# Graph attention with ELU and layer norm on one core: other group sizes, earlier loads, a shorter decode and another order at the end

## What is computed

```python
Wh = x @ W;  We = entity_embs @ W
scores = (Wh @ a1)[:, None] + (We @ a2)[None, :]
e = where(scores > 0, scores, 0.2 * scores)
e = where(adj > 0, e, -9e15)
h = softmax(e, axis=1) @ entity_embs + x
x = layernorm(x + elu(h), axis=-1)
```

## Time and profile before

| | |
|---|---|
| median of 3 runs | 354.25 us (353.78 to 355.08) |
| profiled execution: time | 353.8 us |
| profiled execution: span | 351.7 us |
| busy share of the span: TensorE, VectorE, ScalarE, GpSimd | 80%, 84%, 72%, 12% |
| first fused operation (line 542) starts | 65.57 us |
| last of the 128 is done | 333.48 us |

### The profile page before, as it was taken

The page is one execution under the profiler, slowest core; times in us unless marked ns, Lnnn a source line. Parts: engine busy times, 40 slices in busy tenths (PEclk is TensorE's granted clock), DMA queues, the critical chain, the costliest instruction groups (busy, mean ns, idle before and its releaser), DMA issues.

```text
span 351.7 us, 7943 instructions
## 1 busy us (share of the span) xinstructions
PE 280.9 (80%) x3470; PEld 142.3 (40%) x3470; DVE 296.7 (84%) x356; ACT 253.6 (72%) x216; POOL 40.9 (12%) x45
## 2 busy tenths in 40 slices
PE   1249675779999989999999999999959696667730
PEld 1146454535445544455445445545423232212210
DVE  1780523799988989999999999999999999999944
ACT  1087563399888949999999899999837764646620
POOL 6011110001101000000000310000040000002201
PEclk9998999699999999999999999999999999999985
DMA  7999999999999968887989591000000000000000
GB/s 149 257 207 208 207 207 207 207 208 206 207 175 187 151 101 126 136 131 120 152 140 145 85 173 32 2 3 2 2 0 32 3 0 2 0 2 0 32 0 30
DMA packets 34817, 37.23 MB, mean 106 GB/s; under 512 B 672, under 2 KB 33504, under 8 KB 34784
## 3 DMA queue, kind: packets, MB, share of 16 engines
q0 software_dynamic: 33280, 33.56, 59.0%
q1 hardware_dynamic: 1504, 3.18, 3.2%
HBM read 69.24 MB, written 1.05 MB: 200 GB/s over the span
## 4 chain that ended last, share of the span: by engine, by line
PE 32%; issue 22%; DVE 21%; DMA 13%; ACT 9%; POOL 2%; POOLq 1%; DVEq 0%; ACTq 0%
PE acc L749 12%; DMA raw<-adj_dram 12%; DVE xm L534 10%; PE pairs L698 10%; PE acc L752 6%; DVE wts L542 5%; ACT mask L321 5%; ACT wts L335 3%; PE hist L714 3%; POOL rstd L278 1%; DVE mask L523 1%; PE misc L729 1%; DMA w_sb<-weights_in_dram 1%; ACT drow L351 1%; POOL raw L272 1%
## 5 line engine op out<-in xcount | busy, mean ns | idle before, releaser
L335 ACT ACTIVATE wts<-wts,q_bias 128x1024 f32<-128x1024 f32 x128 | 143.5, 1150 | 45.1 <-DVE wts L542 44.4
L542 DVE SCALAR_TENSOR_TENSOR wts<-pb,q_bend,xm 128x1024 f32<-128x1024 f32 x128 | 160.5, 1279 | 2.0 <-PE acc L752 1.8
L749 PE MATMUL acc<-wts,ent_sb 128*32 128x512 f32 x1024 | 135.4, 601 | 16.8 <-ACT wts L335 13.1
L321 ACT ACTIVATE mask<-pairs 128x2048 bf16<-128x2048 bf16 x53 | 99.0, 1875 | 28.9 <-PE pairs L698 28.9
L698 PE MATMUL pairs<-ident,raw 128*128 128x128 bf16 x1024 | 71.3, 226 | 13.2 <-DMA raw<-adj_dram 10.3
L534 DVE TENSOR_TENSOR xm<-mask,drow 128x2048 bf16<-128x2048 bf16 x64 | 78.1, 1220 | 2.3 <-ACT drow L351 2.3
L752 PE MATMUL acc<-wts,onesf 128*32 128x256 f32 x1024 | 78.6, 379 | 0.0
L698 PEld LDWEIGHTS pairs<-ident,raw 128*128 128x128 bf16 x1024 | 61.6, 102 | 34.3 <-issue 23.0
L752 PEld LDWEIGHTS acc<-wts,onesf 128*32 128x32 f32 x1024 | 33.1, 111 | 77.6 <-issue 77.6
L272 POOL DMA_DIRECT2D raw<-adj_dram x32 | 28.3, 884 | 173.6 <-PE pairs L698 170.9
L749 PEld LDWEIGHTS acc<-wts,ent_sb 128*32 128x32 f32 x1024 | 26.7, 109 | 42.0 <-ACT wts L335 27.9
(11 more groups left out here) (98 smaller groups left out, 101.2 us busy)
## 6 DMA issues: line engine op xcount, KB each, us to landing
raw<-adj_dram POOLq DMA_DIRECT2D x32, 1024.0 KB, 10.5
ent_sb<-ent_blocks_dram SPq DMA_DIRECT2D x1, 1024.0 KB, 7.5
x_sb<-x_dram SPq DMA_DIRECT2D x4, 256.0 KB, 8.6
out_dram<-y SPq DMA_DIRECT2D x4, 256.0 KB, 2.0
w_sb<-weights_in_dram SPq DMA_DIRECT2D x1, 32.5 KB, 2.1
```

The source lines that it names most:

```text
L321: act.activation(mask[:, i % RING:i % RING + 2, 0:n], pairs[j % 2][:, :, 0:n], ACT.Relu, scale=2.0 ** LIFT).then_inc(act_mask_done, 1)
L335: act.activation(part, part, ACT.Exp, bias=q_bias[:, b:b + 1]).then_inc(w_done, 1)
L542: dve.scalar_tensor_tensor(wts[:, i % SLOTS, 0:n], pb[:, P * TILE0[g]:P * TILE0[g] + n], q_bend[:, b:b + 1], xm[:, i % XS, 0:n], ALU.max, ...
L749: pe.matmul(acc[0][to:to + Q, 0:n], ent_sb[:, b, Q * f:Q * f + Q], part[:, n * k:n * k + n], start=(b == 0), stop=(b == NB - 1))
```

## The change

- The groups have 4, 6, 8, 8 and 6 tiles, so there are 160 steps and 40 loads. All operations of a group are as wide as its tiles. Which pairs VectorE masks changes (`by_dve`): pairs 7, 9, 11, 13, 15 of group 0, each second of group 1, pairs 1, 4, 8 and 12 of group 2. Of pair 15 ScalarE and VectorE mask one step each. The last load of the first group is split in two.
- GpSimd issues its first load without waiting for the weights.
- The decode has two operations that don't wait for each other and a minimum, where it had five in a chain; their constants are made in `q_scale` and `find_shift`. `empty` is made behind them.
- For the first group VectorE copies the row to `drow`, in place of ScalarE.
- After the last step, VectorE copies the sums out of PSUM beside ScalarE's copy of the features, takes the positive part beside the exponential, and squares by itself.

```diff
-SIZES = (8, 8, 8, 8)
+SIZES = (4, 6, 8, 8, 6)
...
-            return g == 0 and k >= 9 and k % 2 == 1 or g == 1 and k % 3 == 2 or g == 2 and k in (2, 5)
+            return g == 0 and k >= 7 and k % 2 == 1 or g == 1 and k % 2 == 1 or g == 2 and k in (1, 4, 8, 12)
+
+        def by_act(j):
+            return j == GROUP_PAIRS - 1 or not by_dve(j)
...
+                first = CHUNK // 2 if n == LATE else CHUNK
+                pool.dma_start(raw[:, n % RAWS, 0:SIZES[g], 0:P * first],
+                               rows(adj, g)[:, :, P * CHUNK * c:P * (CHUNK * c + first)]).then_inc(adj_in[n % RAWS], 16)
+                if n == LATE:
+                    pool.dma_start(raw[:, n % RAWS, 0:SIZES[g], P * first:P * CHUNK],
+                                   rows(adj, g)[:, :, P * (CHUNK * c + first):P * CHUNK * (c + 1)]).then_inc(late_in, 16)
...
-            pool.wait_ge(w_in, 16)
             load(0)
...
                 dve.wait_ge(q_step, 6)
+                dve.tensor_scalar(key_slope[:, 0:1], qstep[:, :], -1.0, None, ALU.mult)
+                dve.tensor_scalar(key_slope[:, 1:2], qstep[:, :], -ALPHA, None, ALU.mult)
...
+                dve.tensor_tensor(base_diff[:, :], shift[:, :], qbase[:, :], ALU.subtract).then_inc(shift_step, 1)
+                dve.scalar_tensor_tensor(key_base[:, :], qbase[:, :], -ALPHA, shift[:, :], ALU.mult, ALU.add).then_inc(shift_step, 1)
+                dve.wait_ge(shift_step, 5)
+                dve.tensor_scalar(p_base[:, :], pcol[:, :], ALPHA - 1, base_diff[:, :], ALU.mult, ALU.add).then_inc(shift_step, 1)
...
-                dve.tensor_scalar(empty[:, s], st[:, 3, 0:m], 1.0, None, ALU.is_le)
-                dve.tensor_scalar(st[:, 0, 0:m], st[:, 3, 0:m], qstep[:, :], qbase[:, :], ALU.mult, ALU.add).then_inc(st_step, 1)
...
+                dve.scalar_tensor_tensor(st[:, 0, 0:m], st[:, 3, 0:m], key_slope[:, 0:1], p_base[:, s], ALU.mult,
+                                         ALU.add).then_inc(st_step, 1)
+                dve.tensor_scalar(st[:, 1, 0:m], st[:, 3, 0:m], key_slope[:, 1:2], key_base[:, :], ALU.mult,
+                                  ALU.add).then_inc(st_step, 1)
                 dve.wait_ge(st_step, n + 5)
...
+                dve.tensor_tensor(dcol[:, 0:m], st[:, 0, 0:m], st[:, 1, 0:m], ALU.min).then_inc(d_done, 1)
+                dve.tensor_scalar(empty[:, s], st[:, 3, 0:m], 1.0, None, ALU.is_le).then_inc(empty_done, 1)
...
+            def finish_last():
+                dve.wait_ge(w_used, STEPS)
+                dve.wait_ge(turn_sums_mm, g)
+                dve.tensor_copy(wsum_sb[0:sums, 0:P * fourth(g)], acc[1][0:sums, 0:P * fourth(g)]).then_inc(last_wsum, 1)
+                for part in range(4):
+                    finish(g, part)
+                dve.wait_ge(att_done, NG)
+                fin_inc(dve.scalar_tensor_tensor(pos, y_g, 0.0, x_gr, ALU.max, ALU.add))
+                fin_wait()
+                dve.wait_ge(elu_done, NG)
+                fin_inc(dve.scalar_tensor_tensor(y_g, e_g, 1.0, pos, ALU.min, ALU.add))
+                for part in (6, 7):
+                    finish(g, part)
+                dve.wait_ge(centred, NG)
+                dve.tensor_tensor(e_g, y_g, y_g, ALU.mult).then_inc(square_done, 1)
+                for part in (8, 9, 10):
+                    finish(g, part)
```

More of the change, by code:

```diff
@@ L19 @@
 CHUNKS = STEPS // CHUNK
+LATE = NB // CHUNK - 1
 RAWS = 5
@@ L126, in attention_layernorm @@
         qbase = sb("qbase", [P, 1], fp32)
+        key_slope = sb("key_slope", [P, 2], fp32)
+        key_base = sb("key_base", [P, 1], fp32)
+        base_diff = sb("base_diff", [P, 1], fp32)
+        p_base = sb("p_base", [P, NT], fp32)
         empty = sb("empty", [P, NT], fp32)
@@ L193, in attention_layernorm @@
         d_done = sem("d_done")
+        empty_done = sem("empty_done")
         row_mm = sem("row_mm")
@@ L244, in by_dve @@
             g, k = divmod(j, GROUP_PAIRS)
-            return g == 0 and k >= 9 and k % 2 == 1 or g == 1 and k % 3 == 2 or g == 2 and k in (2, 5)
+            return g == 0 and k >= 7 and k % 2 == 1 or g == 1 and k % 2 == 1 or g == 2 and k in (1, 4, 8, 12)
+        def by_act(j):
+            return j == GROUP_PAIRS - 1 or not by_dve(j)
         def mask_made(engine, j):
-            engine.wait_ge(dve_mask_done if by_dve(j) else act_mask_done, sum(by_dve(k) == by_dve(j) for k in range(j + 1)))
+            if by_act(j):
+                engine.wait_ge(act_mask_done, sum(by_act(k) for k in range(j + 1)))
+            if by_dve(j):
+                engine.wait_ge(dve_mask_done, sum(by_dve(k) for k in range(j + 1)))
         @block.sync
@@ L314, in store_pair @@
                 i = 2 * j
-                if by_dve(j):
+                if not by_act(j):
                     return
@@ L320, in store_pair @@
                 n = cols(i // NB)
-                act.activation(mask[:, i % RING:i % RING + 2, 0:n], pairs[j % 2][:, :, 0:n], ACT.Relu,
+                k = 1 if by_dve(j) else 2
+                act.activation(mask[:, i % RING:i % RING + k, 0:n], pairs[j % 2][:, 0:k, 0:n], ACT.Relu,
                                scale=2.0 ** LIFT).then_inc(act_mask_done, 1)
@@ L358, in take_acc @@
                 rows_of_sums = Q * len(fourths(g))
-                act.activation(acc_sb[:, 0:P * half(g)], acc[0][:, 0:P * half(g)], ACT.Copy)
-                act.activation(wsum_sb[0:rows_of_sums, 0:P * fourth(g)], acc[1][0:rows_of_sums, 0:P * fourth(g)],
-                               ACT.Copy).then_inc(acc_free, 1)
+                features_taken = act.activation(acc_sb[:, 0:P * half(g)], acc[0][:, 0:P * half(g)], ACT.Copy)
+                if g + 1 < NG:
+                    act.activation(wsum_sb[0:rows_of_sums, 0:P * fourth(g)], acc[1][0:rows_of_sums, 0:P * fourth(g)],
+                                   ACT.Copy).then_inc(acc_free, 1)
+                else:
+                    features_taken.then_inc(acc_free, 1)
             for j in range(4):
@@ L522, in store_pair @@
                 n = cols(i // NB)
-                dve.tensor_scalar(mask[:, i % RING:i % RING + 2, 0:n], pairs[j % 2][:, :, 0:n], 2.0 ** LIFT, 0.0, ALU.mult,
-                                  ALU.max).then_inc(dve_mask_done, 1)
+                k = 1 if by_act(j) else 0
+                dve.tensor_scalar(mask[:, i % RING + k:i % RING + 2, 0:n], pairs[j % 2][:, k:2, 0:n], 2.0 ** LIFT, 0.0,
+                                  ALU.mult, ALU.max).then_inc(dve_mask_done, 1)
             def masked(j):
@@ L628, in _ @@
             decode(0)
+            take_row(0)
             dve.wait_ge(p_rows, ROWS)
@@ L644, in _ @@
                         masked(s // 2 + 1)
-            for part in range(11):
-                finish(NG - 1, part)
+            finish_last()
         @block.tensor
@@ L691, in turn_pair @@
                 pe.wait_ge(adj_in[n % RAWS], 16 * (n // RAWS + 1))
+                if j == GROUP_PAIRS - 1:
+                    pe.wait_ge(late_in, 16)
                 if j >= 2:
```

29 lines of the change are left out of this document (16 added, 13 removed).

## The result

The changed kernel takes 347.88 us (median of 4, 347.55 to 349.07) beside 354.01 for the kernel before: ratio 0.9831, 95% interval 0.9802 to 0.986. It is 1.7% faster.

What follows compares the result with a forecast made beforehand. Start and tail cost wide groups, the loop narrow ones, bounded by TensorE in groups 0 and 1, then mostly VectorE. Start -17.2, loop +21.0, tail -3.4 gave +0.4 on the 354.25 median: 354.6 us, range 349.5 to 358.5.

Steps and rivals of the forecast that it cites:

- the surcharge on the loop: Loop: TensorE-bound groups run 3% over the engine's sum; group 0 gets 2.0 over plus 0.7, group 1 gets 1.3.
- The row of a group: TensorE's sums: eight transposes of the row priced at 1.04 us, taken from the start's trace.
- The weight loads behind 128-column sums: Group 0 at 4 tiles: weight loads hide less well behind short sums, 0.7 us, bounded by nothing to 1.5.
- The prices by width: Loop: costs scaled by tiles; weighing a step takes TensorE 1.29 us at 8 tiles, 1.075 at 6, 0.645 at 4.
- The start: Before the first fused operation: it comes at 48.4 us against 65.6, so -17.2, with bounds 46.5 and 51.
- The 137: Start: hardware queue at 137 GB/s with both queues fed, so earlier adj loads make ent land at 10.4, 1.45 late.
- the half clock for two pairs: Start's upper bound, 51 us: TensorE's clock falls in the wait to 33.6, staying low for a third of remaining pairs.
- the entity sum blocks pair 7: Start: pair 7's mask stands behind the 3.87 us ent_part reduction on VectorE, to 33.6, and TensorE waits.
- The tail: After the last step: 14.8 us against 18.2, so -3.4, with bounds 14.2 and 16.
- the shorter decode: VectorE's decode in the loop falls from 2.5 to 2.1 us, included in the group sums.
- Handoffs in group 0: Slower rival: VectorE idles 6.7 us before masks, waits feed each other, group 0 takes 52, total 359.5; chance 0.25.
- The shorter start: Faster rival: ent lands at 8.93 and pairs with a row take 1.2 instead of 1.45: -3.0, total 351.6; chance 0.30.

Runs made afterwards that it cites:

- experiment 2: The changed kernel with four groups of 8 tiles and the old by_dve shares, so all but the sizes: 349.58 us, ratio 0.9866 to the kernel before.
- experiment 9: The kernel before, with VectorE masking pairs 1, 4, 7, 10, 13 of group 1 instead of 2, 5, 8, 11, 14: 353.18 us, ratio 0.9983.
- experiment 1: The kernel before with the new group sizes 4, 6, 8, 8, 6 alone: 349.48 us, ratio 0.9871 to the kernel before.
- experiment 3: The changed kernel with VectorE masking the pairs it masked before (old by_dve shares): 345.66 us, ratio 0.9777 to the kernel before.
- experiment 7: The changed kernel with the old decode, five operations in a chain and empty ahead of them: 350.28 us, ratio 0.9893 to the kernel before.
- Experiment 10: The changed kernel with pair 7 of group 0 masked by ScalarE and group sizes 4, 8, 8, 8, 4: 342.18 us, ratio 0.966 to the kernel before.
- experiment 4: The changed kernel with the ent_part reduction cut in three, behind the masks of pairs 7, 9 and 11: 343.50 us, ratio 0.9706 to the kernel before.
- experiment 5: The changed kernel with the mask of pair 7 of group 0 back on ScalarE, other shares new: 343.83 us, ratio 0.9712 to the kernel before.
- experiment 8: The changed kernel with the old tail: both copies on ScalarE, old order of parts, squares on ScalarE: 349.12 us, ratio 0.9846 to the kernel before.
- experiment 12: The kernel before, with VectorE masking pairs 0, 3, 6, 9, 12, 15 of group 1 instead of 2, 5, 8, 11, 14: 355.02 us, ratio 1.002.
- experiment 6: The kernel of experiment 4 with two pairs of group 1 turned early, between spreading and row of group 0: 346.38 us, ratio 0.9771 to the kernel before.

## Why the prediction was wrong

**The step that failed is the surcharge on the loop.** The text took TensorE's sum for group 0 of the kernel before, 69.2, and the measured 71.2, and said: "TensorE-bound groups run 3% over the sum." It then put 2.0, 1.3, 1.2 and 0.6 over the sums of groups 0 to 3, and 0.7 for weight loads: 5.8 us in all, from one group of another width. Against the sums without surcharge the five groups of the changed kernel came out at +0.6, -1.5, +0.7, -0.4 and -0.3, 1.0 us under on the whole. So 5.8 of the 6.8 us are the surcharge, and the rest is the sums themselves.

**Where the excess had come from.** By the windows, TensorE is idle for 3.98 us in group 0 before (71.24 less 67.26) and for 0.43 in group 0 after (45.79 less 45.36). Before, 2.9 of them are two waits for masks at the head of the group, and 0.9 is a wait for the decode near its end; after, a single wait at the head is left. TensorE's timeline of the kernel before, then of the changed kernel:

```profile
72.27 1.05 PE L698 MATMUL pairs<-ident,raw 128*128 128x128 bf16 x16 [2.62 <-ACT mask L321]
...
75.07 1.05 PE L698 MATMUL pairs<-ident,raw 128*128 128x128 bf16 x16 [0.32 <-ACT mask L321]
...
128.67 0.62 PE L736 MATMUL misc<-ident,dcol 128*128 128x128 bf16 x8 [0.91 <-DVE dcol L512]
```

```profile
53.03 0.83 PE L754 MATMUL pairs<-ident,raw 128*128 128x128 bf16 x12 [0.43 <-ACT mask L340]
```

At the head TensorE turns two pairs at once and then needs the first one's mask. ScalarE makes that mask behind its first exponentials, in 1.86 us at 8 tiles and 1.43 at 6. The turning behind the wait starts 6.70 after the first fused operation with groups of 8 (the kernel before, experiments 2 and 9) and 4.24 or 4.25 in every run with 4 and 6 tiles, with old shares or new and at half clock or full ahead of it, though the wait itself is anything from 0.4 to 1.1 there. So the head is set by the width, through this chain, and not by `by_dve`; the length of the wait is only what TensorE has left over in it. The wait near the end is another matter: with narrow groups it is 2.0 and 1.4 with the old shares (experiments 1 and 3), 0.3 with the old decode and the new shares (experiment 7), and gone with both new.

How the two add up to 2.0 is argued, not shown. The clock is a rival that no run removes. It does not explain why the excess went, since its mean was lower in the changed kernel's group 0 (0.96, for 0.99 before). But it seems to count: in experiment 2 the waits are 2.3 and 0.3, 1.3 us less than before, and group 0 is still 0.6 longer, with a granted clock of 0.83 from 67 to 77 us, where the kernel before has 0.95 and then 1.00.

**The second miss is a price read at the wrong clock.** The row of a group went into TensorE's sums at 1.04 us, from the start, where the granted clock is 0.50 (62 to 67 us). In the loop the row of 8 tiles starts 0.45 ahead of what follows it (128.67 to 129.12 in group 0 of the kernel before), and that of 6 tiles 0.35 (88.51 to 88.86 in the changed kernel). That is 0.5 to 0.6 a group. The spreading, taken as equal, was right: 1.03 in the loop at 8 tiles and 0.82 at 6. Of group 1's 1.5 under its sum the row is 0.6; about 0.9 stays open (the boundaries are VectorE's, which can be a step more or less ahead of TensorE).

The weight loads behind 128-column sums, put at 0.7 us, cost nothing that shows. From the sums to the next start it takes 0.22 us, where 128 columns at the forecast's 1.68 ns make 0.215 (TensorE's timeline in group 0 of the changed kernel):

```profile
63.01 0.60 PE L805 MATMUL acc<-wts,ent_sb 128*32 128x256 f32 x8
63.44 0.39 PE L808 MATMUL acc<-wts,onesf 128*32 128x128 f32 x8
63.66 0.34 PE L770 MATMUL hist<-mask,codes 128*32 128x384 bf16 x4
```

**The prices by width were right.** Weighing at 4 tiles is 0.65 here (63.01 to 63.66), for 0.645. In group 1 of the changed kernel two steps and a pair take 3.50, for 2 x 1.075 + 1.35:

```profile
125.75 1.07 PE L754 MATMUL pairs<-ident,raw 128*128 128x128 bf16 x16
...
129.25 1.07 PE L754 MATMUL pairs<-ident,raw 128*128 128x128 bf16 x16
```

Group 4 is 49.69 for 50.0, group 3 64.67 for 65.1 without surcharge. Experiment 10 was forecast by the bare sums before it ran, and its loop came 1.3 us over them (its span 0.7), where the surcharges would have put it 3 to 5 higher.

**The start was right by luck: two errors cancel.** `ent_sb` was there at 9.25, not 10.4. Both queues had work from 4 us on. From 6 to 8 us of the changed kernel they moved (packets, MB, share of 16 engines):

```profile
q1 hardware_dynamic: 86, 0.34, 71.2%
q0 software_dynamic: 104, 0.11, 34.7%
```

The hardware queue moved 0.34 MB in 2 us, 170 GB/s and as much as in the kernel before, not 137. The 137 was misread: in the first of the 3 us of the earlier trace rows the hardware queue moved only 0.04 MB, and 0.37 in the next two. The forecast had cited the Trainium skill (DMA: Bandwidth & Descriptors, Queues, rings and completion order) for turns by packet. The trace agrees: 86 packets stand beside 104. But those of the hardware queue carry 4.0 KB each and the others 1.1, so equal turns gave it three quarters of the bytes.

Against the early `ent_sb` stood the half clock for two pairs, which the forecast had only as its upper bound. The seven pairs behind the wait take 9.6 us from the first turning to the last (32.66 to 42.25), where 1.40 each would make 8.4. That the entity sum blocks pair 7 was foreseen in place and size, but taken as the price of the start; it was a mishap of the shares, worth 3.9 us (experiments 4 and 5).

**The tail was right**, 14.6 for 14.8, its order 1.26 for 1.45 (experiment 8). The worth of the shorter decode was put too low: the forecast gave it 0.4 a group where VectorE bounds, and 2.1 came out in all (experiment 7).

**The rivals.** Handoffs in group 0 (0.25): VectorE waited 2.3 us before its masks there, not 6.7, and the group was shorter than forecast, not longer. The point of this rival, 359.5, also lay above the end of the stated range, 358.5. The shorter start (0.30) had the sign right and the place wrong. No case had a loop at its bare sums. Each carried the surcharge on, and so the range ended 1.6 us above the time.

## What to carry to other kernels

An excess of a stage over its fullest engine's sum is not a rate to carry to stages of other widths: look in the waits for the places where it arose, and ask whether the change keeps them. Take each price at the clock at which the stage will run. And when work is shared out anew between two engines, look at what stands ahead of it in the new engine's queue: one mask behind a 3.9 us reduction cost 3.9 us, where the whole change gained 6.2.

## What the runs showed of the hardware

The granted clock of TensorE was at half behind waits of 1.98 us (experiment 1), 2.26 (experiment 2), 3.14 (experiment 12) and 3.22 (the changed kernel), but not behind each: it stayed up behind 2.62 in the kernel before. Experiment 2 has that same wait for the same mask, and there the turning behind it runs at half clock:

```profile
70.35 1.86 PE L754 MATMUL pairs<-ident,raw 128*128 128x128 bf16 x16 [2.26 <-ACT mask L340]
```

The wait of 3.2 us for pair 7 was followed by turnings of 1.01 us in one execution and of 0.61 in another, and the start differed by 1.4 us with it. Filling a wait of 1.86 us with work (experiment 6) left 0.53 of it and brought one of 1.94 behind it, and the granted clock was at half for the same 5 us (0.50, and 0.52 without the edit).

Two DMA queues with work at the same time moved nearly equal numbers of packets (86 and 104 from 6 to 8 us), and bytes by the size of their packets (0.34 and 0.11 MB).
